# Two attention stages: values at the end of the following step, one fill matmul per step, images written out, one burst per stage

## The reference, cut to what matters

```
# window stage: for each shift in (0, 2) and each half of the channels, 8 heads of 8 channels,
# strips of 128 positions (w = window, h = head)
attn = softmax(einsum('whqc,whkc->whqk', qw, kw), axis=-1)
ow = einsum('whqk,whkc->whqc', attn, vw) + lw
...
# token stage: n = 1024 tokens, 16 heads of 8 channels
attn = einsum('bhqd,bhkd->bhqk', q, k)
attn = softmax(attn, axis=-1)
out = einsum('bhqk,bhkd->bhqd', attn, v)
...
return out @ w_proj + b_proj
```

## Time and profile before

| | |
|---|---|
| median of 3 runs | 4560.41 us (4534.22 to 4561.75) |
| the profiled execution | 4556.71 us |
| its span, first to last instruction | 4554.6 us |
| mean granted clock of TensorE | 0.918 |
| PE busy | 3870.5 us (85%) |
| DVE busy | 2549.4 us (56%) |
| ACT busy | 1923.6 us (42%) |
| POOL busy | 840.2 us (18%) |

### The profile page before, as it was taken

How to read it: one execution, slowest core, us unless ns; L and a number is a source line. 1 busy time by engine, 2 the same in 40 slices (tenths; PEclk the granted TensorE clock), 3 DMA queues, 4 the chain that set the end, 5 groups by cost and what they waited for, 6 DMA issues and landing times. The chain is left out here.

```text
span 4554.6 us, 74651 instructions
## 1 busy us (share of the span) xinstructions
PE 3870.5 (85%) x25243; PEld 1648.1 (36%) x25243; DVE 2549.4 (56%) x4085; ACT 1923.6 (42%) x2321; POOL 840.2 (18%) x861
## 2 busy tenths in 40 slices
PE   7988888847698989898999999876997838999999
PEld 4655555524322212121222222224346723444444
DVE  3246555546577777777777777723447622333333
ACT  1215454511146565555555565643432312232332
POOL 0002222310000000000000000000430004555555
PEclk9989787978789999999999999987999859999999
DMA  4443343300400000000000000001430012322221
GB/s 142 133 109 88 91 88 85 80 16 2 165 9 14 18 14 18 13 18 14 18 14 20 12 23 18 4 8 56 151 102 1 0 72 80 94 83 76 97 81 48
DMA packets 137582, 247.79 MB, mean 54 GB/s; under 512 B 34808, under 2 KB 47264, under 8 KB 136800
## 3 DMA queue, kind: packets, MB, share of 16 engines
q1 hardware_dynamic: 137312, 243.98, 18.9%
HBM read 171.55 MB, written 56.62 MB: 50 GB/s over the span
## 5 line engine op out<-in xcount | busy, mean ns | idle before, releaser
L1071 DVE TENSOR_REDUCE mxv<-mx_ps 128x1 f32<-128x512 f32 x2048 | 1315.2, 685 | 413.8 <-PE mx_ps L931 413.5
L1046 ACT ACTIVATE PT<-st_ps 128x1024 f32<-128x1024 f32 x1024 | 1003.6, 1022 | 710.7 <-PE st_ps L943 710.5
L931 PE MATMUL mx_ps<-KS,QS 24*128 24x512 f16 x2048 | 731.7, 397 | 30.3 <-DMA QS<-qk 16.4
L957 PE MATMUL o_ps<-PT,VA 128*32 128x512 f32 x4096 | 559.6, 618 | 159.2 <-ACT PT L1046 107.9
L1914 DVE TENSOR_TENSOR u<-h_ps,s 128x512 f32<-128x512 f32 x352 | 243.3, 691 | 541.4 <-ACT s L1889 492.7
L1951 POOL TENSOR_TENSOR hg<-u,gb 128x512 f32<-128x512 f32 x352 | 451.5, 1284 | 378.7 <-DVE u L1914 300.9
L666 DVE TENSOR_REDUCE mxv<-mx_ps 128x4 f32<-128x512 f32 x512 | 332.9, 685 | 231.8 <-PE mx_ps L542 229.5
L1889 ACT ACTIVATE s<-h_ps 128x512 f32<-128x512 f32 x352 | 210.2, 597 | 595.4 <-PE h_ps L1863 595.4
L368 PE MATMUL st_ps<-KS,ident 128*128 128x512 f16 x1024 | 406.0, 396 | 6.8 <-ACT TX L1036 6.2
L1871 PE MATMUL y_ps<-hg,w 128*128 128x512 f32 x704 | 360.7, 596 | 56.3 <-POOL hg L1951 56.2
L943 PE MATMUL st_ps<-QS,KS 26*128 26x512 f16 x2048 | 404.4, 392 | 0.0
(11 more groups left out here) (231 smaller groups left out, 4399.0 us busy)
## 6 DMA issues: line engine op xcount, KB each, us to landing
gb<-g SPq DMA_DIRECT2D x64, 512.0 KB, 3.7
gb<-g SPq DMA_DIRECT2D x16, 2048.0 KB
QK<-qk SPq DMA_DIRECT2D x128, 192.0 KB
qk<-hl SPq DMA_DIRECT2D x80, 256.0 KB, 3.3
RB<-d SPq DMA_DIRECT2D x48, 256.0 KB, 3.5
qk<-hl SPq DMA_DIRECT2D x64, 128.0 KB, 3.3
v<-vs SPq DMA_DIRECT2D x32, 256.0 KB, 3.2
VS<-v SPq DMA_DIRECT2D x32, 256.0 KB, 3.1
```

The costliest lines, as they stand in the source:

```text
L931: nc.tensor.matmul(mx_ps[:, use % 3, :], rows(QS, g // 2, j, STACK)[:, t * C:(t + 1) * C], rows(KS, g // 2, j, STACK)[:, half * HALF:(half ...
L957: mm = nc.tensor.matmul(o_ps[32 * j:32 * j + 32, :], VA[:, g // 2 % 2, kt, j, :], PT[:, n % 2, j, :], start=(kt == 0), stop=(kt == KT - 1))
L1046: nc.scalar.activation(PT[:, n % 2, 2 * a:2 * a + 2], st_ps[:, a], ACT.Exp, scale=1.0 / SHIFT ** 2).then_inc(st_free[a], 1)
L1071: nc.vector.tensor_reduce(mxv[:, g % 2, j, t, half:half + 1], mx_ps[:, slot], AX.X, ALU.max).then_inc(mx_free, 1)
```

## The change

It makes four edits, in both stages alike. The values of step n - 1 stand behind both halves of step n. The fill stands only in the first half of a step. Each half runs its scores first and then both its look-ahead matmuls. All eight images are written out, and the burst of `warm_up` stands in the first image alone. The other engines keep their order, with the loop written out.

```diff
         def periods(engine, image):
             image(0, "first")
-            with engine.Fori(1, LAST) as i:
+            for i in range(1, LAST):
                 image(i, "mid")
             image(LAST, "last")
...
                 def scores(n, a):
                     g, kt = n // KT, n % KT
-                    fill_array(nc, st_ps[:, a, 1], ident, KS[:, g // 2, 0:HALF])
+                    if a == 0:
+                        fill_array(nc, st_ps[:, a, 1], ident, KS[:, g // 2, 0:HALF])
...
                         for a, pair in enumerate(PAIRS):
-                            ahead(pair[0])
                             pe.wait_ge(st_free[a], i * st_per(a) + (st_use(n, a, kind) + 1))
-                            if n == WARM_AT and a == 0:
+                            if n == WARM_AT and a == 0 and kind == "first":
                                 warm_up(nc, st_ps[:, a, 0], identf, X)
                             scores(n, a)
-                            ahead(pair[1])
+                            for j in pair:
+                                ahead(j)
                             if a:
                                 continue
...
-                            if n:
-                                values(i, n - 1, kind)
-                            elif kind != "first":
-                                values(i - 1, STEPS - 1, "mid")
+                        if n:
+                            values(i, n - 1, kind)
+                        elif kind != "first":
+                            values(i - 1, STEPS - 1, "mid")
```

More of the change, by code:

```diff
@@ L552, in scores @@
                     u, s = n // 4, n // 2 % 2
-                    fill_array(nc, st_ps[:, a, 1], ident, KS[:, u, s, 0:HALF])
+                    if a == 0:
+                        fill_array(nc, st_ps[:, a, 1], ident, KS[:, u, s, 0:HALF])
                     for w in range(4):
@@ L617, in image @@
                                     turn(use)
-                            if n:
-                                values(i, n - 1)
-                            elif kind != "first":
-                                values(i - 1, STEPS - 1)
+                        if n:
+                            values(i, n - 1)
+                        elif kind != "first":
+                            values(i - 1, STEPS - 1)
                 periods(pe, image)
```

## The result

| | before | after |
|---|---|---|
| median of the runs | 4556.75 us (4534.22 to 4561.75) | 4230.13 us (4221.34 to 4239.76) |
| the profiled execution | 4556.71 us | 4227.69 us |
| its span | 4554.6 us | 4225.8 us |
| mean granted clock | 0.918 | 0.925 |
| instructions | 74651 | 66475 |

After to before is 0.9293 (95% interval 0.9255 to 0.9331): 7% faster. A run more than 1.5% above the fastest of its kernel is left out of the ratios here; e12_values_only has three such runs of 11 and e10_qk_early one of four.

A forecast was written before the change was run, and what follows sets the result against it. It took a ring through the exponential, 3.14 us a warm token step, as the bound. From 4556.7 us it took 250 (token stage) and 115 (window stage): 4192, stated as 4195 us, range 4090 to 4430.

The forecast's parts named there:

- V: The values matmuls of a step; before, they waited for the exponential, and that wait was to go.
- A: A look-ahead matmul whose row maximum VectorE takes; the fourth of a step was to wait for the step's first reduction.
- The token step: Warm step of the token stage, bound by the three-buffer ring of the maxima: 2.80 us against 3.14.
- F: The full-array fill; removing the second of a step was held to be worth nothing there.
- S: A pair of score matmuls; starts .32 us after the fill, a change of tiling, and runs beside the look-ahead matmuls.
- rival 3: Row groups do not run four at a time: step 3.01 us, 108 more in the token stage, 4300; chance .08.
- The token image: One token-stage image: 64 steps of 2.80 plus 6.1, with 2.5 for clock falls: 188 us; stage 250 less.
- The clock: Steady steps no danger, only waits; falls end unaided within a few steps, a low step taking 4.32 us against 4.98.
- this rival: The clock stays down in the token stage after a fall at the first projection: 4900 us; chance .08 in full.
- The window stage: Steps of 2.80 us plus a 7 us wait and clock falls: 60 us a steady image, 467 against 582.6, 115 less.
- The round: Window stage: from storing DEN through DMA and POOL to the split maxima, 28.1 us, not shortened by the change.
- rival 4: VectorE already bounds the step if the fourth look-ahead matmul precedes the values: 2.40 us, 205 less, 3990; chance .06.

The follow-up runs named there:

- e12_values_only: The kernel before with only the values moved behind both halves; loops, bursts and both fills stay: 4548.16 us, ratio 0.9958.
- e10_qk_early: The changed kernel with the window stage's loads of queries and keys issued earlier, ahead of the denominators: 4216.09 us, ratio 0.9232.
- e4_bursts: The changed kernel with the burst of five full-array matmuls put back into every image: 4296.44 us, ratio 0.9423.
- e6_loops: The changed kernel with the hardware loops kept in both stages: 4292.75 us, ratio 0.9397.
- e2_order: The kernel before with only the new order of scores, look-ahead matmuls and values; loops, bursts and both fills stay: 4328.93 us, ratio 0.9482.
- e3_fill2: The changed kernel with the fill put back into the second half of each step: 4243.79 us, ratio 0.9309.
- e5_nofill: The changed kernel with no fill at all: 4707.87 us, ratio 1.0324.
- e7_rows_first: The changed kernel with the window stage's row loads issued ahead of the loads of queries and keys: 4256.17 us, ratio 0.9337.
- e1_unroll: The kernel before with only the loops over the images written out, in both stages: 4487.74 us, ratio 0.9837.
- e8_fourth: The changed kernel with the fourth look-ahead matmul of each step moved behind the values, both stages: 4050.69 us, ratio 0.8883.

## Why the prediction was right, point by point

**What bounds.** Right. The exponential was the link that the change cut: e12_values_only, in which the values alone move, has the warm step of 2.82 us against 3.14, and the changed kernel 2.85. In the changed kernel the wait before V is gone and the one before the fourth A has come, put down to VectorE.

**The token step.** Forecast 2.80 as .42 + .73 + .32 + 1.00 + .32, measured 2.85 as .46 + .75 + .32 + .99 + .33. Every link is within .04. The change from row tiles to column tiles, for which I had no row free of a wait, is the .32 that I borrowed from F to S. Four row groups do run together: the first pair of scores and two look-ahead matmuls start at 1980.05, the second pair and the third look-ahead matmul .23 later. The Trainium skill ("TensorE: Matmul & The Clock Gate", Part 3) would, by the estimate in the prediction, have had a group of four take .28 us. The trace does not agree with that: it shows .23, near the .21 used. So rival 3 fell.

**The token image.** Forecast 188, measured 191.2. The step makes 64 x .05 = 3.2 of that. The surplus beyond 64 steps is 191.2 - 182.4 = 8.8; I had 6.1, and 2.5 for a fall in four images of ten. No fall came, and the turn steps and the projection are dearer: a turn step is 3.45, eight of them .6 more each, and the step across the projection 6.04 instead of 2.85. Together 8.0 of the 8.8. I also took 5.9 us off for the burst, and e4_bursts prices it at 4.3. So errors of opposite sign met: the step and the surplus too low by some 6 us, a fall of 2.5 that didn't come. That the image is within 3 us is in part luck. With seven such images the stage lost 232 us where I had 250.

**The clock.** I expected the fall to undo itself because the low step is denser than before's. In the changed kernel nothing fell in the token stage, so it shows nothing; e4_bursts and e6_loops show it: falls of 3 to 31 us that end without a burst, with a low step of 4.37 where I had 4.32. e12_values_only shows the other side: with nearly the same warm step, but one A ahead of each half, the low step is 4.98 and nothing ends the fall but the burst. e2_order, with the same fills and bursts, comes back. So the order of S and A decides it, as I expected; that it does so by packing the work more densely fits, but no run shows that by itself. I gave this rival too little thought in one respect: the fill. I called the second F free and was right (e3_fill2). I also wrote that steady steps are no danger, only a wait is, and e5_nofill shows steady steps of 2.53 us that lose the clock with no longer wait than the changed kernel has in every step. With one F left that case didn't arise, so the forecast didn't suffer.

**The window stage.** Forecast 115 less, measured 105. Mean of the six middle images 62.4, forecast 60. The size was right and the mechanism not. I had PE wait for the split maxima at the turn of step 13 and of step 5. The round is as long as I said: DEN stored at 506.64, `RB<-d` issued at 518.51, POOL at 525.90, the split ready at 534.34, 27.7 us against 28.1; this is the round that ends in step 5, where the forecast followed the one that ends in step 13. But PE stops earlier, at the fills of steps 4 and 12, for the rows `QK<-mT`, issued at 522.83 behind the large load of queries and keys. By the time those rows let it go, at 531.66, the split is nearly done, and its turn in step 5 waits for nothing on POOL. So that the size came out is luck. I had named `QK<-mT` among the waits to look for and priced the wrong one. Of the 40.7 us in twelve waits, 39.7 lie in the six middle images, 6.6 us each, where I had 7. e7_rows_first and e10_qk_early show that the order of SP's queue matters, by 26 us one way and some 14 the other. Why the first of them made it worse is argued and not shown: an issue that waits for the turn holds back all that is behind it, but e10_qk_early has such waits too (24.7 us in 11) and got faster.

**The parts.** What I had as separate terms overlap. The new order alone gives 228 us (e2_order), and the writing out 69 alone (e1_unroll) and 63 on top (e6_loops). The bursts cost 66 (e4_bursts); I had 5.9 us for one in the token stage, and it is 4.3 in an image without a fall. The second fill costs between 0 and 14. The longer program, costed at nothing, has made the step .10 longer in the order of before (e1_unroll). I had taken the written-out first and last images of before as the reason to cost it at nothing, and their steps of 3.24 us were there to be read. In the new order, in which V doesn't wait for the exponential, the step is 2.84 to 2.85 with the loop and without, so the error had no effect.

**The rest.** 9 us of the saving went outside the two stages: 3.9 between them and 6.2 behind them. I had nothing for that and no experiment looked at it.

**What rival 4 was worth.** It did not happen by itself: V stays behind the fourth A on PE, as it is written (1981.58 and 1981.26). And it was the best thing to do on purpose: e8_fourth takes 180 us off. The prediction had 3990 for it, from steps of 2.40 with all else as forecast. Measured are 2.48 and 4051, of which 35 are the forecast's own error.

## What to carry to other kernels

Write a step down as the ring that closes it, link by link, and ask of each edit which link it takes out and which ring is next; here that gave the step within .05 us, and the next ring (one look-ahead too early in the queue) named the following 180 us. Then ask what a step costs at half clock and whether such steps end the fall by themselves: two orders with warm steps of 2.82 and 2.84 us, alike in all else, are worth 9 and 228 us (e12_values_only, e2_order). A matmul whose result nobody reads may be what holds the clock, so take it out alone, once, before calling it free.

## What the runs showed of the hardware that I had not expected

- **A fall needs no wait.** In e5_nofill the clock drops 34 us after the burst in running steps and stays at 1.2 GHz for the stage; with one full-array matmul in each step, of 2.85 us, the changed kernel keeps its clock through the stage.
- **Being busy does not bring the clock back.** In e12_values_only PE is busy 214.19 of 215.00 us at 0.50. In e4_bursts and e6_loops, with PE busy 15.77 of 17.00 and 12.73 of 14.00, it comes back. It comes back in e2_order too, which has both fills and the bursts of e12_values_only. The low steps differ in what runs beside what: four row groups at once in those that come back. Whether that is the cause, or something else in the order, is not shown.
- **The same wait, two outcomes.** A wait of 1.21 us at the projection is followed by a fall four times in seven in e4_bursts and never in the changed kernel; one of .89 us four times in seven in e12_values_only and never in before. What decides it stays open.
